# Order of VectorE's work within a part of a graph network's first layer: its additions and next one-hots ahead of its counting work instead of behind it

## The chip, the cores and the metric

The kernel runs on one core of a Trainium2 chip. Its time is the device time of one execution in microseconds (us). Lower is better. The engines are called as in the profile: PE is TensorE (its weight loads are PEld), DVE is VectorE, ACT is ScalarE, POOL is GpSimd and SP is SyncE, which only issues transfers.

## The reference, cut to what matters

A graph of 12,500 nodes with 128 features and 200,000 edges, sorted by destination, goes through a layer norm with ReLU and then three SAGE layers (128 to 256 to 256 to 128 features). Batch norm and ReLU stand between the layers, and the input is added to the result.

```python
def _sage_conv(x, src, dst, Wl, bl, Wr):
    agg = jax.ops.segment_sum(x[src], dst, num_segments=x.shape[0])
    deg = jax.ops.segment_sum(jnp.ones_like(dst, dtype=x.dtype), dst, num_segments=x.shape[0])
    mean = agg / jnp.maximum(deg, 1.0)[:, None]
    return mean @ Wl + bl + x @ Wr
```

The sum over edges is most of the work. The change concerns the stretch in which the first layer's sums are made.

## The kernel before, in words

**Two ways to sum.** Destinations are so skewed that the first nodes get most edges. For them the kernel counts, once, how many edges go from each source to each destination. This table, `edge_count`, is made in `HBS` = 46 strips of 64 destinations. It then multiplies the node features by the counts ("dense"). The remaining edges are walked in tiles of 128: POOL gathers 128 rows of the node table by an indirect DMA into `ring` (line 698), PE multiplies the rows by a 128x32 one-hot matrix of where each edge goes (`sum_part`, line 929), and DVE adds the 32 resulting columns into the sums in `big` (`accumulate`, line 1268).

**Bodies and parts.** In the first layer, 52 bodies of 4 parts of 5 tiles are worked through. `ring` and `onehot` have room for one body. Part g of body i+1 takes the place of part g of body i as soon as PE has multiplied the latter: ACT then copies the next indices (`stage_indices`, line 802), POOL gathers with them, and DVE writes the next one-hots (`hots`, lines 1243 and 1261). PE alternates between two PSUM banks for its products, so its product for a part waits for the additions of the part two before it.

**What rides along.** Each part of the first layer's bodies also carries a slice of other work, named `counting`:

- Bodies 0 to 8: nothing in the parts; DVE and PE make tables between the bodies.
- Bodies 9 to 35 (108 parts): the counts. DVE makes two f16 one-hot matrices for each step, in batches of at most 8 steps (`count_hots`, line 1399, two instructions a batch). They go into 16 slots. PE multiplies them, one matmul a step (`count_edges`, line 943), and ACT copies the result out of PSUM (line 815). Before a batch of slots is overwritten, DVE waits for PE to have done the steps that were in them (`s_count_step`), and PE waits for the batch (`s_count_hot`). There are 2208 steps: the first 8 parts have 48, 24, 20, 16, 14, 14, 12 and 12; then come 4 parts of 24, 8 of 20, 8 of 16, 48 of 24 and 32 of 16.
- Bodies 36 to 51: the dense product (`first_dense`, line 964, in 49 parts, the first of body 36 to the first of body 48) on PE, and the degrees. For these, DVE makes the hots in every second part (`window_degrees`, lines 1290, 1243, 1293 and 1296, in parts 0 and 2), and PE multiplies them in parts 1 and 3 (`sum_degrees`, line 951).

**Order on the engines.** Each engine has its own program, in order, tied to the others by semaphores. In a part, PE does `sum_part` and then its counting matmuls. DVE does its counting one-hots, then loads five window positions into registers (`nodes_of`, line 1271), then the five additions, each waiting for PE's `sum_part` of the same part or for the addition before, and then the next one-hots. In a part g, DVE's `accumulate` waits as follows, and `hots` waits for the same semaphore value:

```python
                if j == 0:
                    dve.wait_ge(s_sum[layer], i * PARTS + (g + 1))
```

The other two layers use `add_parts` with a `counting` that does nothing. An irregular-input branch is not taken with these inputs.

Of the kernel before, what the change touches and what calls it, by code (L numbers as in the profile page):

```python
# [78 lines left out]
def gnn_kernel(nc, x, src, dst, Wl0, bl0, Wr0, g0, b0, Wl1, bl1, Wr1, g1, b1, Wl2, bl2, Wr2, out):  # L79
# [10 lines left out]
    with ctx:  # L90
# [1070 lines left out]
        def _(dve):  # L1161
# [78 lines left out]
            def one_hots(out, numbers, values):  # L1240

                n, w = values.shape[1], numbers.shape[1]
                return V.tensor_tensor(out, numbers.rearrange("p (a w) -> p a w", a=1).to_broadcast([P, n, w]),  # L1243
                                       values.rearrange("p (n a) -> p n a", a=1).to_broadcast([P, n, w]), ALU.is_equal)

            def hots(layer, i, g):
                if not (isinstance(i, int) and i == 0):

                    dve.wait_ge(s_sum[layer], i * PARTS + (g + 1 - PARTS))
                n = PER_PART[layer]  # L1250
                rel = rel_all[:, ds(i * PER_BODY[layer] + (FIRST[layer] + g * n), n)]
                one_hots(onehot[:, g * n:(g + 1) * n, :], iota_row[:, 0:W], rel).then_inc(s_hot[layer], 1)

            def accumulate(layer, i, g, j, node):
                n = PER_PART[layer]
                if j == 0:
                    dve.wait_ge(s_sum[layer], i * PARTS + (g + 1))
                k = g * n + j

                if not (isinstance(i, int) and i == 0 and k == 0):  # L1260
                    dve.wait_ge(s_acc[layer], i * PER_BODY[layer] + k)
                step = part_ps(layer, g, j)
                if layer == 1:
                    sums = big[:, 0:2, ds(node, W)]
                    step = step.rearrange("p (m c) -> p m c", c=W)
                else:
                    sums = big[:, 1 if layer == 0 else 0, ds(node, W)]
                V.tensor_tensor(sums, sums, step, ALU.add).then_inc(s_acc[layer], 1)  # L1268

            def nodes_of(first, count, most):  # L1270
                _, values = nc.values_load_multi_w_load_instructions(  # L1271
                    node_row[0:1, ds(first, count)], engines=[mybir.EngineType.DVE], min_val=0, max_val=most,
                    skip_runtime_bounds_check_because="a window starts at a node or a block, and at most where it ends with the last")
                return values
# [25 lines left out]
            def add_parts(layer, i, counting=lambda g: None, last=False):  # L1300
                n = PER_PART[layer]
                for g in range(PARTS):
                    counting(g)
                    nodes = nodes_of(i * PER_BODY[layer] + (FIRST[layer] + g * n), n, PADDED - W)
                    for j in range(n):
                        accumulate(layer, i, g, j, nodes[j])
                    if not last:
                        hots(layer, i + 1, g)

            def hots_of_first(layer):  # L1310
                for g in range(PARTS):
                    hots(layer, 0, g)
# [93 lines left out]
            def body_0(i, counting):  # L1406
                add_parts(0, i, counting, last=isinstance(i, int) and i == BODIES[0] - 1)
                if isinstance(i, int):
                    if i == 0:
                        say_irregular()  # L1410
                        tables_for_picks()
                        window_nodes()
                    if i == 1:
                        mark_reached()
                    if i == 2:
                        dve.wait_ge(s_steps, 1)
                        link(V.scalar_tensor_tensor(out=tile_row, in0=flat_ps[:, 3 * 512:3 * 512 + STEP_COLS], scalar=1.0,
                                                    in1=tile_row, op0=ALU.max, op1=ALU.add))
                        pick(0)
                    if 3 <= i < 3 + len(STEP_CHUNKS):  # L1420
                        keep_codes(i - 3)
                        if i - 2 < len(STEP_CHUNKS):
                            pick(i - 2)
                    if i == 2 + len(STEP_CHUNKS):
                        link(V.reduce_sum(tally[:, 0:1], tally[:, 2:2 + len(STEP_CHUNKS)], mybir.AxisListType.X))
                        V.tensor_tensor(tally[:, 7:8], tally[:, 1:2], tally[:, 0:1], ALU.subtract).then_inc(s_insides, 1)
                    if i == TABLE_BODIES - 1:
                        dve.wait_ge(s_total, 1)
                        V.tensor_scalar(outside[:, :], ps[:, 3, 0:1], float(EDGES), None, ALU.add).then_inc(s_outside, 1)
# [119 lines left out]
            def sum_edges(layer):  # L1549
                hots_of_first(layer)  # L1550
                dve.wait_ge(s_zero[layer], (CHUNKS + 1) // 2)
                dense_bodies(dve, layer, lambda i, units, last: add_parts(layer, i, last=last))
                dve.wait_ge(s_acc[layer], BODIES[layer] * PER_BODY[layer])
                with if_irregular(dve):
                    dve.wait_ge(s_dense, dense_kept(layer))
                    link(V.memset(big[:, 0:3 - layer, :], 0.0), s_sort)
                    sum_late(layer)
                dve.sem_inc(s_summed, 1)
# [64 lines left out]
```

## Time and profile before

| | before |
|---|---|
| median of 3 runs | 4572.26 us (4563.02 to 4572.82) |
| the profiled execution | 4568.78 us |
| its span in the trace | 4567.0 us |
| mean granted PE clock over the span | 0.852 of full |
| PE, DVE, ACT, POOL busy | 3538.9, 1965.2, 665.2, 3180.7 us |
| first counting one-hots of DVE | 369.48 us into the span |
| last counting matmul of PE begins | 1377.6 us into the span |

### The profile page before, as it was taken

The numbers are of one execution on the slowest core, as the hardware profiler recorded it, in microseconds if no ns is written. First come the engines' busy times: TensorE is split into PE (matmuls) and PEld (weight loads), VectorE is DVE, ScalarE is ACT, GpSimd is POOL, SyncE is SP. The second block draws the span as 40 slices with busy tenths as digits, with TensorE's granted clock in tenths as the row PEclk, the third lists the DMA queues.
The fourth block names the chain that finished last, engine by engine and source line by source line (L and its number), as shares of the span: only waits on it lengthen the run. The fifth ranks groups of instructions, "written<-read, shape, count | busy, mean of one in ns | idle before, by whom it ended". The sixth has DMA issues, their size and how long they took to land.

```text
span 4567.0 us, 62659 instructions
## 1 busy us (share of the span) xinstructions
PE 3538.9 (77%) x16020; PEld 2298.8 (50%) x16020; DVE 1965.2 (43%) x5344; ACT 665.2 (15%) x1712; POOL 3180.7 (70%) x3027
## 2 busy tenths in 40 slices
PE   3356766666668996889999999999885888888876
PEld 1233433333434554776666666666583444444446
DVE  4546867878766777532222222222361222222212
ACT  3001234444440000420000000000030000000002
POOL 2778887777887777037777777777725777777774
PEclk6567878878778996999999999999897888888887
DMA  5212345445569995187677677777669888888886
GB/s 170 65 52 72 121 158 196 189 183 208 227 233 276 290 290 144 74 270 205 203 203 207 199 213 203 203 203 203 206 202 248 214 221 218 214 214 224 213 229 185
DMA packets 928868, 896.10 MB, mean 196 GB/s; under 512 B 62823, under 2 KB 832505, under 8 KB 921754
## 3 DMA queue, kind: packets, MB, share of 16 engines
q1 hardware_dynamic: 819210, 643.90, 47.9%
q0 software_dynamic: 106432, 250.27, 19.0%
q10 hardware_dynamic: 3152, 1.06, 0.1%
q8 instruction: 33, 0.54, 0.0%
q14 instruction: 41, 0.34, 0.0%
HBM read 683.01 MB, written 211.98 MB: 196 GB/s over the span
## 4 chain that ended last, share of the span: by engine, by line
PE 35%; issue 15%; POOL 14%; DMA 12%; DVE 11%; SPq 8%; DVEq 3%; ACT 1%; POOLq 0%; ACTq 0%
POOL ring L698 14%; PE ps L1083 14%; PE ps L929 11%; DMA ring<-table,idx_now 9%; SPq L537 6%; DVE area L1399 5%; PE ps L943 2%; DVE big L1268 2%; PE ps L1125 2%; PE ps L1110 2%; DVEq L1271 2%; DMA table<-area 1%; PE ps L1153 1%; PE ps L1056 1%; PE ps L1063 1%
## 5 line engine op out<-in xcount | busy, mean ns | idle before, releaser
L698 POOL DMA_INDIRECT ring<-table,idx_now x2836 | 3026.7, 1067 | 1051.7 <-issue 924.7
L1268 DVE TENSOR_TENSOR big<-big,ps 128x32 f32 (+1 forms) x2836 | 566.4, 200 | 2205.2 <-PE ps L929 1808.2
L929 PE MATMUL ps<-onehot,ring 128*128 128x32 f32 x7632 | 1023.7, 288 | 495.9 <-DMA ring<-table,idx_now 281.2
L929 PEld LDWEIGHTS ps<-onehot,ring 128*128 128x128 f32 x7632 | 1030.5, 210 | 733.8 <-issue 711.4
L1083 PE MATMUL ps<-area 128*128 128x512 f32 (+1 forms) x2744 | 1380.1, 649 | 25.1 <-DMA area<-table 24.2
L1083 PEld LDWEIGHTS ps<-area 128*128 128x128 f32 x2744 | 553.8, 214 | 564.3 <-issue 539.7
L943 PE MATMUL ps<-area 128*128 128x392 f16 x2208 | 518.2, 395 | 230.1 <-DVE area L1399 228.1
L1399 DVE TENSOR_TENSOR area<-iota_code,area 128x3136 f16<-128x3136 f16 (+4 forms) x568 | 648.8, 1204 | 57.7 <-PE ps L943 53.5
L802 ACT ACTIVATE idx_now<-idx_all 128x5 int32 (+3 forms) x608 | 125.1, 207 | 3034.4 <-PE ps L929 3019.9
L943 PEld LDWEIGHTS ps<-area 128*128 128x128 f16 x2208 | 237.1, 115 | 479.5 <-DVE area L1399 272.0
L815 ACT ACTIVATE big<-ps 128x392 f32<-128x392 f32 x736 | 350.8, 499 | 419.9 <-PE ps L943 418.4
L964 PE MATMUL ps<-big 128*128 128x512 f32 x444 | 203.1, 607 | 22.6 <-DMA big<-table 22.6
L737 POOL MEMSET big<- 128x512 f32 (+2 forms) x50 | 36.2, 725 | 252.7 <-ACT ring L850 252.7
L1243 DVE TENSOR_TENSOR onehot<-iota_row,rel_all 128x160 f32<-128x160 f32 (+1 forms) x608 | 190.5, 315 | 16.2 <-issue 5.0
L964 PEld LDWEIGHTS ps<-big 128*128 128x128 f32 x444 | 82.5, 192 | 115.9 <-issue 109.5
L1125 PE MATMUL ps<-ring,w 128*128 128x256 f32 x392 | 86.9, 385 | 19.8 <-DMA ring<-input 19.8
L1296 DVE TENSOR_SCALAR area<-iota_code,area,wrong 128x98 f16<-128x98 f16 x416 | 94.3, 330 | 4.2 <-DVE wrong L1293 2.0
L1110 PE MATMUL ps<-w,ring 128*128 128x256 f32 x392 | 86.3, 384 | 7.6 <-ACT ring L850 7.6
L1125 PEld LDWEIGHTS ps<-ring,w 128*128 128x128 f32 x392 | 75.8, 194 | 31.2 <-issue 20.5
L1520 DVE BATCH_NORM_STATS2 stats<-big (+2 forms) x196 | 72.8, 414 | 28.5 <-ACT big L835 28.2
L1110 PEld LDWEIGHTS ps<-w,ring 128*128 128x128 f32 x392 | 75.5, 193 | 18.4 <-issue 8.0
L850 ACT ACTIVATE ring<-big,bn_shift,bn_scale 128x512 f32 (+2 forms) x100 | 74.3, 796 | 61.6 <-DMA input<-ring 44.8
(138 smaller groups left out, 1418.7 us busy)
## 6 DMA issues: line engine op xcount, KB each, us to landing
edge_count<-big SPq DMA_DIRECT2D x46, 3136.0 KB
area<-edge_count SPq DMA_DIRECT2D x98, 1472.0 KB
area<-edge_count SPq DMA_DIRECT2D x98, 960.0 KB
big<-edge_count SPq DMA_DIRECT2D x37, 1536.0 KB, 10.0
ring<-table,idx_now POOLq DMA_INDIRECT x2836
area<-table SPq DMA_DIRECT2D x98, 256.0 KB
ring<-input SPq DMA_DIRECT2D x98, 256.0 KB, 2.7
input<-ring SPq DMA_DIRECT2D x48, 512.0 KB, 3.8
```

The costliest lines, as they stand in the source:

```text
L537: sp.dma_start(first_rows[b], tb0[:, ds(unit * 2, 2), :]).then_inc(s_unit[b], 16)
L698: pool.indirect_dma_start(out=ring[:, g * n + j, 0:width], out_offset=None, in_=table[layer][:, :], in_offset=bass.IndirectOffsetOnAxis(ap ...
L815: nc.scalar.activation(count_half[:, half, :, k * GN:(k + 1) * GN], ps[:, 4 + k % 4, 0:CODES].rearrange("p (s n) -> p s n", n=GN), ACT.Cop ...
L929: last = nc.tensor.matmul(to[:, m * W:(m + 1) * W], ring[:, k, m * P:(m + 1) * P], onehot[:, k, :], start=True, stop=True)
L943: nc.tensor.matmul(ps[:, 4 + k % 4, 0:CODES], low_hot[:, slot % SLOTS, :], code_hot[:, slot % SLOTS, :], start=(c == 0), stop=(c == caps[k ...
L964: last = nc.tensor.matmul(first_dense_ps(b)[:, 0:wide].rearrange("p (h c) -> p h c", c=HB), first_rows[g][:, s, :], first_counts[g][:, at ...
L1083: last = nc.tensor.matmul(dense_ps(layer, f, k)[:, 0:(end - h) * HB].rearrange("p (h c) -> p h c", c=HB), unit_rows[b][layer][:, s, f * P: ...
L1110: last = nc.tensor.matmul(ps[:, u, j * HID:(j + 1) * HID], h_stage[:, u, k, j * P:(j + 1) * P], w1[:, 0, k, :], start=(k == 0), stop=(k == 1))
L1125: last = nc.tensor.matmul(ps[:, u, m * CH:(m + 1) * CH], w1[:, 1, k, m * P:(m + 1) * P], own1[:, u, k, :], start=(k == 0), stop=(k == 1))
L1243: return V.tensor_tensor(out, numbers.rearrange("p (a w) -> p a w", a=1).to_broadcast([P, n, w]), values.rearrange("p (n a) -> p n a", a=1 ...
L1268: V.tensor_tensor(sums, sums, step, ALU.add).then_inc(s_acc[layer], 1)
L1399: ins = V.tensor_tensor(hots[:, at:at + count, :].rearrange("p s (n a) -> p s n a", a=2), iota_code[:, 0:w].rearrange("p (b n a) -> p b n ...
```

## The change

In `add_parts`, `counting(g)` is moved from ahead of the loads, additions and next one-hots of part g to behind them. Only DVE's program changes; the programs of PE, ACT, POOL and SP, all waits and all instructions stay the same. For bodies 9 to 35, `counting` is `count_hots`, and for bodies 36 to 51 it is `window_degrees` in parts 0 and 2; elsewhere it does nothing.

```diff
             def add_parts(layer, i, counting=lambda g: None, last=False):
                 n = PER_PART[layer]
                 for g in range(PARTS):
-                    counting(g)
                     nodes = nodes_of(i * PER_BODY[layer] + (FIRST[layer] + g * n), n, PADDED - W)
                     for j in range(n):
                         accumulate(layer, i, g, j, nodes[j])
                     if not last:
                         hots(layer, i + 1, g)
+                    counting(g)
```

## Rows read from the trace of the kernel before

**Rows 1.** Busy time by stage; columns: stretch, length, engines (instructions), clock, DMA share, GB/s

```profile
369.40:434.60 65.20, 49.22 (x240) 29.25 (x240) 55.68 (x98) 9.11 (x23) 53.34 (x39) 0.79 0.15 39
434.60:610.50 175.90, 113.27 (x582) 68.58 (x581) 133.74 (x225) 43.42 (x99) 145.43 (x101) 0.80 0.36 129
610.50:1112.80 502.30, 324.15 (x1641) 183.14 (x1638) 393.16 (x577) 201.33 (x434) 386.00 (x257) 0.83 0.49 187
1112.80:1375.80 263.00, 163.58 (x822) 104.44 (x822) 187.22 (x321) 116.74 (x283) 216.38 (x147) 0.80 0.61 232
1375.80:1728.90 353.10, 326.96 (x1358) 183.02 (x1357) 242.65 (x673) 12.51 (x54) 265.20 (x250) 0.97 1.15 289
```

**Rows 2.** Who waited for whom, stretch 660 to 1112 us, parts of 24 steps

```profile
PE ps L943 <- DVE area L1399: 158.2, 104, 4.0
DVE big L1268 <- issue: 47.7, 22, 2.4
```

**Rows 3.** Who waited for whom, stretch 1201 to 1376 us, parts of 16 steps

```profile
PE ps L929 <- DMA ring<-table,idx_now: 30.4, 5, 6.3
```

**Rows 4.** Timeline, 1000 to 1040 us: start, length, engine, line, operation

```profile
1001.52 4.69 DVE L1399 TENSOR_TENSOR area<-iota_code,area 128x1024 f16<-128x1024 f16 x4
...
1003.97 4.55 PE L943 MATMUL ps<-area 128*128 128x392 f16 x16 [2.08 <-DVE area L1399]
...
1008.86 1.50 DVE L1268 TENSOR_TENSOR big<-big,ps 128x32 f32 x5
...
1010.33 1.20 PE L929 MATMUL ps<-onehot,ring 128*128 128x32 f32 x10
...
1010.63 6.99 DVE L1399 TENSOR_TENSOR area<-iota_code,area 128x1024 f16<-128x1024 f16 x6
...
1019.02 1.20 PE L929 MATMUL ps<-onehot,ring 128*128 128x32 f32 x10
1019.74 1.51 DVE L1268 TENSOR_TENSOR big<-big,ps 128x32 f32 x5 [2.12 <-issue]
...
1021.52 4.69 DVE L1399 TENSOR_TENSOR area<-iota_code,area 128x1024 f16<-128x1024 f16 x4
...
1023.97 4.94 PE L943 MATMUL ps<-area 128*128 128x392 f16 x16 [3.76 <-DVE area L1399]
...
1030.83 1.20 PE L929 MATMUL ps<-onehot,ring 128*128 128x32 f32 x10
```

**Rows 5.** Counting matmuls, one line of the kernel: shortest, median and longest in ns

```profile
L943 PE MATMUL ps<-area x2208: 326/329/535, 373.2 to 1377.6; 128*128 128x392 f16 x184
```

**Rows 6.** Timeline, 1215 to 1255 us, parts of 16 steps

```profile
1223.09 2.00 POOL L698 DMA_INDIRECT ring<-table,idx_now  x1 [0.30 <-issue]
...
1231.85 2.34 PE L929 MATMUL ps<-onehot,ring 128*128 128x32 f32 x10 [6.01 <-DMA ring<-table,idx_now]
...
1234.41 1.51 DVE L1268 TENSOR_TENSOR big<-big,ps 128x32 f32 x5 [3.76 <-PE ps L929]
```

**Rows 7.** Timeline, 1500 to 1530 us, dense product and degrees

```profile
1501.89 1.20 PE L929 MATMUL ps<-onehot,ring 128*128 128x32 f32 x10
...
1503.32 1.51 DVE L1268 TENSOR_TENSOR big<-big,ps 128x32 f32 x5 [2.34 <-PE ps L929]
...
1509.40 1.25 PE L929 MATMUL ps<-onehot,ring 128*128 128x32 f32 x10
...
1522.67 0.89 PE L951 MATMUL ps<-area 128*98 128x128 f16 x13
```

**Rows 8.** Timeline, 1738 to 1760 us, degrees without a dense product

```profile
1742.95 1.08 DVE L1290 TENSOR_SCALAR area<-area,iota_row 128x1664 f16<-128x1664 f32 x1
...
1750.64 1.62 PE L951 MATMUL ps<-area 128*98 128x128 f16 x13 [6.42 <-DVE area L1296]
...
1752.05 2.34 PE L929 MATMUL ps<-onehot,ring 128*128 128x32 f32 x10
...
1754.95 1.28 DVE L1290 TENSOR_SCALAR area<-area,iota_row 128x1664 f16<-128x1664 f32 x1
```

## The prediction

> **What bounds the kernel now.** I read the busy time by stage first, cutting the span where DVE begins the one-hots of another kind of part. The counting bodies 9 to 35 are the first four stretches and last 65.2 + 175.9 + 502.3 + 263.0 = 1006.4 us for 108 parts [rows 1]. There DVE is busy 71 to 85% of the time, PE 62 to 76%, POOL 77 to 83%. No engine is full, so the next view is who waits for whom. In the parts of 24 steps, which take 502.3 / 48 = 10.5 us each, PE waits for the counting one-hots (158.2 us in 104 waits), and DVE waits 47.7 us in 22 waits for nothing but its own issue, ahead of the additions: the register load [rows 1, 2]. In the parts of 16 steps, 263.0 / 32 = 8.2 us each, PE waits for gathered rows [rows 1, 3]. Then comes the timeline, to see who overlaps with whom. PE makes a part's product at 1010.33; DVE begins the same part's counting one-hots at 1010.63 and adds the product at 1019.74, 9.4 us after it was made [rows 4]. The reader is to see that the additions hardly ever wait for PE here, because PE has the product ahead of the counting matmuls. That is why DVE can go on without pause: while PE works off up to 16 slots, DVE adds and starts the next part's one-hots. After them, in bodies 36 to 48, PE is busy 326.96 of 353.1 us at clock 0.97, and is the bound [rows 1].
>
> **What the change does in bodies 9 to 35.** No instruction is added or removed, and none on another engine moves. Let S be PE's product of a part, P its counting matmuls, A the additions, H the next one-hots, C the counting one-hots. PE's order is S P, S P. DVE's was C A H; it becomes A H C. A(g) needs S(g), S(g) stands behind P(g-1) on PE, and P(g-1) needs C(g-1). So after its last batch of C, DVE must wait until PE has worked off all the slots and made S, and only then add; meanwhile nothing for P(g) is made, and PE in turn waits through A, H and the first batch of C. The two engines overlap only inside C and P. The part becomes one chain:
>
> - A and H: from the start of the additions to that of the one-hots, 1010.63 - 1008.86 = 1.77 us [rows 4].
> - The first batch: PE starts 1003.97 - 1001.52 = 2.45 us after DVE (again 2.45 at 1021.52) [rows 4].
> - The matmuls. In these two instances PE had been waiting 2.08 and 3.76 us, as it will in each part now (1.77 + 2.45 is 4.2 us), and 16 of them took 4.55 and 4.94 us [rows 4]. The third batch must wait for slots of the first. From the start of C to the next S, 24 steps took 1010.33 - 1001.52 = 8.81 and 1030.83 - 1021.52 = 9.31 us; I take the mean, 9.06. Without the third batch it is 2.45 + 4.75, less 0.1 because matmul ends are modelled: 7.1. Four steps more at the upper clock add 0.67.
> - S until A can start: 1503.32 - 1501.89 = 1.43 us [rows 7].
>
> So a part takes 1.77 + 9.06 + 1.43 = 12.26 us for 24 steps, 10.3 for 16 and 10.97 for 20. A step fewer than 16 takes off 4.75 / 16 = 0.3: 9.7 for 14 and 9.1 for 12. The 48-step part adds three batches at DVE's pace of 6.99 / 3 = 2.33 [rows 4], 19.3. By stretch, against rows 1:
>
> - First 8 parts: 19.3 + 12.26 + 10.97 + 10.3 + 2 x 9.7 + 2 x 9.1 = 90.4, before 65.2: +25.2.
> - 4 of 24, 8 of 20, 8 of 16: 219.2, before 175.9: +43.3.
> - 48 of 24: 588.5, before 502.3: +86.2.
> - 32 of 16: 329.6, before 263.0: +66.6.
>
> Together +221.3 us. This is net of what goes away: the stalls for the register load fall into the wait for P and S (3.1 us from the end of C to A, against at most about 2.2 for the load), and the waits for rows vanish since the gathers have time: in the last stretch they average 216.38 / 147 = 1.47 us with 0.30 between, 8.9 us for five [rows 1, 6], under 10.3. That cover is thin: a gather beside DVE's one-hots took 2.00 us [rows 6], and five such would be 11.5 us. But the one-hots fill less of a longer part than before. DVE's reads of PSUM sooner release PE's banks sooner, which nobody waits for: costed at nothing, below nothing excluded, because no wait for the banks is among the large ones.
>
> By the Trainium skill (SBUF — State Buffer, on which ops grab the shared pair), a tensor_tensor of DVE should not hold up GpSimd's descriptors, as the page infers; the gather of 2.00 us beside line 1399 disagrees. By the page POOL would leave more room still, and the sum would be the same.
>
> **The bounds of the clock's share.** At the upper level throughout, a matmul goes at half of the 0.327 us that rows 5 show as the common duration. C to S is then 2.45 + 2 x 2.33 + 1.3 = 8.4 us for 24 steps, 6.1 for 16, 6.75 for 20: parts of 11.6, 9.3 and 9.95 us, together +133. At the lower level throughout, matmuls take 0.327 each and S to A 1234.41 - 1231.85 = 2.56 us [rows 5, 6]: parts of 14.6, 12.0 and 13.3 us, together +448. I take the mixture because two instances with nearly this idle time show it.
>
> **Bodies 36 to 51.** In parts 0 and 2, `window_degrees` now starts after A and H. S at 1509.40 lets A start at 1510.83 and the work at 1512.6; it lasts 1750.64 - 1742.95 = 7.7 us, so it ends at 1520.3, and the consumer on PE stands at 1522.67 [rows 7, 8]. With 2.3 us to spare PE's dense product hides it: 0 (if a register load of 2.2 us fell ahead of A it would still do). If that cover were gone, the price would be the excess, twice in each of 12 bodies: a microsecond is 24 us. Where the dense product has ended (some 7 pairs of parts, to the end of body 51) there is no cover. From the end of the work, PE's degree matmuls take 1752.05 - 1750.64 = 1.41, S until A 2.56, A and H 1.7, the work 7.7: 13.4 us, against 1754.95 - 1742.95 = 12.0 us before [rows 6, 8]. The difference is between 0 and 1.4; I take 1.0, +7, less 2 for the additions that no longer stand behind the last of this work. Bodies 0 to 8 and the other layers have no counting in their parts: 0.
>
> **Sum.** 221.3 + 7 - 2 = +226 us on the profiled execution's 4568.8: 4795. Its time was 3.5 below the median of the runs, so 4798.
>
> **Rivals.**
> - *Upper clock.* PE gets the upper level despite pauses of 4 us: +133 + 5, 4710. For it: even after a pause the 16 matmuls take less than the 5.2 us of the lower level. Against it: they take 4.94 us, not 2.6, after 3.76 us of waiting [rows 4].
> - *Lower clock.* PE never leaves the lower level, as its work comes in pieces: +448 + 5, 5025. For it: a median of 0.329 us, and 2.34 us for S after a wait of 6.01 [rows 5, 6]. Against it: the products after the counting matmuls take 1.20 [rows 4]. The Trainium skill (TensorE: Matmul & The Clock Gate, "What's actually happening") has the clock throttled by default and released by activity; with the new pauses that rule speaks for this rival.
> - *The gathers set the pace.* If the chain were shorter than POOL's pace, nothing would change: 4572. That needs parts of 16 steps at 8.2 us and of 24 at 10.5, where even the upper clock gives 9.3 and 11.6.
> - *Faster.* The register load ahead of A moves out of DVE's way. It cost 47.7 us in 22 waits [rows 2]; for 26 of the 52 parts of 24 steps that is 26 x 2.17 = 56 us: 4516. It decides only if A's new wait for P and S is shorter than what the load cost, about 1.1 us a part; I find 3.1.
>
> **How the numbers follow.** Mixed clock 0.64 (4740 to 4890), upper 0.14, lower 0.10, gathers 0.05, faster 0.04, and 0.03 for something slower outside these. I predict 4798. The range of 4700 to 4920 holds the first two and leaves the rest out. A difference of 0.2% (9 us) is about what can be told from no change: faster 0.04, same 0.05, slower 0.91.
>
> **What would show it.** In the profile after: the counting stretch lasts about 1228 us instead of 1006; parts of 24 steps 12.3 us, of 16 steps 10.3; DVE's largest waits are additions waiting for PE's product (line 929), some 3 us in every part; PE waits about 4 us for each first batch; POOL waits for ACT's indices in most parts; the register load no longer shows; PE still at 0.97 in the dense bodies. It would be wrong if PE's clock settles at one level, or if the degree work in bodies 36 to 48 comes late for PE.

## The result and the profile after

The changed kernel took 4814.41 us at the median (4811.03 to 4816.63) against 4572.28 us before: a ratio of 1.0534, interval 1.0516 to 1.0552. The prediction was 4798 us, 226 us of loss; the measured loss is 242 us. The profiled execution took 4811.03 us with a span of 4809.2 us, 242.2 us more than the span of before.

First, the same view as [rows 1]: busy time by stage, each stretch cut where DVE begins the one-hots of another kind of part. Columns: stretch, length, busy time of PE, PEld, DVE, ACT and POOL with their instructions, granted clock, DMA share, GB/s.

```profile
375.10:467.40 92.30, 55.79 (x240) 30.91 (x240) 56.25 (x96) 9.61 (x24) 64.97 (x52) 0.70 0.17 50
467.40:690.40 223.00, 133.69 (x584) 74.71 (x584) 135.13 (x225) 43.93 (x100) 130.38 (x101) 0.71 0.28 100
690.40:1286.30 595.90, 356.82 (x1632) 194.09 (x1632) 396.87 (x577) 200.89 (x432) 314.42 (x241) 0.77 0.41 156
1286.30:1615.50 329.20, 186.14 (x832) 106.74 (x832) 187.84 (x322) 127.44 (x288) 205.49 (x161) 0.67 0.50 188
1615.50:1977.40 361.90, 333.04 (x1408) 187.38 (x1408) 248.82 (x695) 10.16 (x49) 267.02 (x247) 0.97 1.13 285
```

The reader is to see three things. The four counting stretches have grown from 65.2, 175.9, 502.3 and 263.0 us to 92.3, 223.0, 595.9 and 329.2. DVE's work has not (396.87 us in the third, before 393.16 us). PE's has, with the same work, since its clock fell from 0.83 to 0.77 in the third stretch and from 0.80 to 0.67 in the fourth. The dense stretch that follows is at 0.97, as before.

Who waited for whom, 720 to 1280 us, parts of 24 steps (total us, times, longest), to be held against [rows 2]:

```profile
PE ps L943 <- DVE area L1399: 224.2, 77, 4.6
POOL ring L698 <- ACT idx_now L802: 209.1, 45, 4.9
DVE big L1268 <- PE ps L929: 127.3, 45, 3.1
```

In 45 parts DVE's additions now wait 127.3 / 45 = 2.83 us for PE's product, the new wait. PE waits for DVE in turn, and POOL for the indices of the next gathers, 45 times. Before, the additions' large wait was the register load; it is gone from the list.

The timeline of the same kernel, 1150 to 1192 us, shows one whole part (start, length, engine, line):

```profile
1160.50 1.51 DVE L1268 TENSOR_TENSOR big<-big,ps 128x32 f32 x5 [2.87 <-PE ps L929]
...
1162.28 4.69 DVE L1399 TENSOR_TENSOR area<-iota_code,area 128x1024 f16<-128x1024 f16 x4
...
1164.73 4.45 PE L943 MATMUL ps<-area 128*128 128x392 f16 x16 [4.46 <-DVE area L1399]
...
1167.70 2.39 DVE L1399 TENSOR_TENSOR area<-iota_code,area 128x1024 f16<-128x1024 f16 x2 [0.72 <-PE ps L943]
...
1170.15 1.50 PE L943 MATMUL ps<-area 128*128 128x392 f16 x8 [0.97 <-DVE area L1399]
...
1171.49 1.20 PE L929 MATMUL ps<-onehot,ring 128*128 128x32 f32 x10
...
1172.92 1.52 DVE L1268 TENSOR_TENSOR big<-big,ps 128x32 f32 x5 [2.83 <-PE ps L929]
```

This is the chain of the prediction: from the additions to the one-hots 1.78 us, from the start of the one-hots to the product 9.21 (2.45 of it until PE has the first batch), from the product to the next additions 1.43. Together 12.42 us, where 12.26 were forecast. PE stands idle 4.46 us at the head of this part, 4.39 and 4.46 at the heads of its neighbours.

In the parts of 16 steps (timeline, 1455 to 1495 us) the cycle is 10.24 us, from 1460.27 to 1470.51, where 10.3 were forecast:

```profile
1460.27 1.51 DVE L1268 TENSOR_TENSOR big<-big,ps 128x32 f32 x5 [3.77 <-PE ps L929]
...
1464.50 4.75 PE L943 MATMUL ps<-area 128*128 128x392 f16 x16 [4.46 <-DVE area L1399]
...
1470.51 1.50 DVE L1268 TENSOR_TENSOR big<-big,ps 128x32 f32 x5 [3.77 <-PE ps L929]
```

In these parts PE waited for gathered rows before [rows 3]; now the gathers are on time and the chain sets the pace.

### The profile page after: what moved, and what is told of

It reads as the page before. It is cut to its first block, busy times and chain, and to the rows that moved or that the text cites. A ratio compares the mean times of both kernels' runs of the same rounds, so it can differ in the third digit from the quotient of the medians.

```text
span 4809.2 us, 62646 instructions
## 1 busy us (share of the span) xinstructions
PE 3623.5 (75%) x16020; PEld 2322.8 (48%) x16020; DVE 1969.7 (41%) x5344; ACT 674.2 (14%) x1712; POOL 3088.4 (64%) x3027
## 4 chain that ended last, share of the span: by engine, by line
PE 47%; issue 12%; DVE 11%; POOL 10%; DMA 8%; SPq 7%; DVEq 4%; ACT 1%; POOLq 0%; ACTq 0%
PE ps L1083 14%; PE ps L929 13%; PE ps L943 11%; POOL ring L698 9%; SPq L537 6%; DMA ring<-table,idx_now 5%; DVE area L1399 5%; DVE big L1268 3%; DVEq L1271 2%; PE ps L1125 2%; PE ps L1110 2%; DMA table<-area 1%; PE ps L1153 1%; PE ps L1056 1%; DVEq L1268 1%
## 5 line engine op out<-in xcount | busy, mean ns | idle before, releaser
L698 POOL DMA_INDIRECT ring<-table,idx_now x2836 | 2934.3, 1035 | 1376.6 <-issue 893.0
L929 PEld LDWEIGHTS ps<-onehot,ring 128*128 128x128 f32 x7632 | 1014.0, 207 | 589.3 <-issue 567.5
L929 PE MATMUL ps<-onehot,ring 128*128 128x32 f32 x7632 | 1001.7, 285 | 360.7 <-DMA ring<-table,idx_now 197.2
L943 PE MATMUL ps<-area 128*128 128x392 f16 x2208 | 618.5, 457 | 508.0 <-DVE area L1399 507.4
L943 PEld LDWEIGHTS ps<-area 128*128 128x128 f16 x2208 | 267.8, 128 | 825.7 <-DVE area L1399 464.3
```

The source lines that it names most:

```text
L698: pool.indirect_dma_start(out=ring[:, g * n + j, 0:width], out_offset=None, in_=table[layer][:, :], in_offset=bass.IndirectOffsetOnAxis(ap ...
L929: last = nc.tensor.matmul(to[:, m * W:(m + 1) * W], ring[:, k, m * P:(m + 1) * P], onehot[:, k, :], start=True, stop=True)
L943: nc.tensor.matmul(ps[:, 4 + k % 4, 0:CODES], low_hot[:, slot % SLOTS, :], code_hot[:, slot % SLOTS, :], start=(c == 0), stop=(c == caps[k ...
```

## The experiments

The kernel before was measured again beside the experiments (medians of 4564.08 us for 1 to 4, 4566.97 for 5 to 7 and 4565.45 for 8 and 9), and each ratio is against that. For each kernel, besides its ratio, the *counting stretch* is given: from the first to the last start of a counting matmul in the profiled execution. Before, it is 1377.6 - 373.2 = 1004.4 us [rows 5]; in the changed kernel 1612.3 - 377.4 = 1234.9 us, 230.5 more:

```profile
L943 PE MATMUL ps<-area x2208: 326/531/534, 377.4 to 1612.3; 128*128 128x392 f16 x184
```

The median matmul now takes 531 ns, before 329.

**1. Only the counts behind.** Each part has two places for its work, phase 0 ahead of the additions and phase 1 behind them. The counting one-hots are made in phase 1 alone; the degree work is done in phase 0 alone, by the same kind of test where it is called.

```diff
                 for g in range(PARTS):
+                    phase[0] = 0
                     counting(g)
...
                         hots(layer, i + 1, g)
+                    phase[0] = 1
+                    counting(g)
...
             def count_hots(groups, step, hb, half, caps):
+                if phase[0] == 0:
+                    return
```

> Only the counting one-hots (bodies 9 to 35) go behind the additions; the degree work stays ahead of them. The chain theory puts nearly all of the loss here: the counting matmuls began 4.2 us later and ended 235 us later in the changed kernel, so about 4805 us. The rival, that the degree work is what comes late for PE, gives close to 4572.

Measured: 4803.39 us, ratio 1.0528 (1.0510 to 1.0546). The counting stretch is 1612.4 - 377.6 = 1234.8 us, that of the whole change to 0.1 us. The loss sits in the counting bodies.

**2. Only the degrees behind.** The same, with the two kinds of work exchanged.

> Only the degree work of bodies 36 to 51 goes behind the additions. The chain theory gives about 10 us, all of it in the last three bodies, where no dense product hides it: 4582 us. If the degree work were late for PE in bodies 36 to 48 too, it would be tens of us more.

Measured: 4573.45 us, ratio 1.0020 (1.0010 to 1.0030), so 9 us of loss: small, but the interval leaves out 1. The profiled execution was the longest of the ten, 14 us above the median, so its rows are used for where the loss sits and not for its size. In the rows of the degree matmuls before (first) and in this kernel (second), the last one starts at 1826.7 and 1837.1 us, while counting ended 1.2 us earlier here:

```profile
L951 PE MATMUL ps<-area x416: 217/219/344, 1412.4 to 1826.7; 128*98 128x128 f16 x139
```

```profile
L951 PE MATMUL ps<-area x416: 217/219/345, 1410.1 to 1837.1; 128*98 128x128 f16 x139
```

The last dense matmul starts at 1737.6 us here against 1739.5 before. So bodies 36 to 48 lose nothing, and the loss is behind them, as forecast. The ratios of 1 and 2 add up to that of the whole change (5.28% + 0.20%, against 5.34%, within the intervals).

**3. Next one-hots ahead, additions behind.** This asks whether the additions' work or the wait for PE makes the loss.

```diff
                 for g in range(PARTS):
+                    if not last:
+                        hots(layer, i + 1, g)
                     counting(g)
                     nodes = nodes_of(...)
                     for j in range(n):
                         accumulate(layer, i, g, j, nodes[j])
-                    if not last:
-                        hots(layer, i + 1, g)
```

> Next one-hots ahead of the counting work, additions behind it. The one-hots wait for the same product of PE as the additions, so DVE still stands idle through PE's tail, but the 1.5 us of additions leave the chain. The chain theory gives 12.4 - 1.5 = 10.9 us for a part of 24 steps and 8.8 for one of 16, so 108 x 1.5 = 160 us less than the changed kernel: 4655 us. If only the additions' own wait mattered, it would be as before, 4572; if the place of the one-hots alone mattered, as the changed kernel, 4814.

Measured: 4619.09 us, ratio 1.0115 (1.0099 to 1.0132). The counting stretch is 1426.3 - 381.2 = 1045.1 us, 190 less than in the changed kernel, where 160 were expected. Merely moving the 0.33 us one-hots ahead costs about 1%, because they wait for the same product (the degree work stands behind them here too; behind one-hots and additions it was 0.2% in 2). Most of the loss is gone with the additions' work off the chain. The wait (timeline, 900 to 925 us):

```profile
902.20 0.33 DVE L1243 TENSOR_TENSOR onehot<-iota_row,rel_all 128x160 f32<-128x160 f32 x1 [1.34 <-PE ps L929]
...
904.91 1.50 PE L943 MATMUL ps<-area 128*128 128x392 f16 x8 [2.88 <-DVE area L1399]
```

PE's wait is 2.88 us here instead of 4.46, and after it the first 8 matmuls take 1.50 us, the time of the upper clock level. This does not hold in every part: in the next one, 16 matmuls take 5.26 us after a wait of 3.19. The granted clock is 0.82 from 700 to 1100 us and 0.80 from 1170 to 1400, where the changed kernel has 0.77 in its parts of 24 steps and 0.67 in those of 16. That is where the additional 30 us come from as I read it, though this kernel does not test the clock by itself. The next one does.

**4. The changed kernel with PE kept at work.** Each counting part has 20 matmuls on constants ahead of its counting matmuls, into a bank that is free then; the results are not used.

```diff
+            low_fill, code_fill = iota_code[:, 0:P], iota_code[:, 0:CODES]
+            FILL = 20
+
             def count_edges(groups, step, hb, half, caps):
                 n = sum(caps[k] for k in groups)
+                for _ in range(FILL):
+                    nc.tensor.matmul(ps[:, 2, 0:CODES], low_fill, code_fill, start=True, stop=True)
```

> The changed kernel with 20 matmuls of 392 columns on constants in each counting part, ahead of the part's counting matmuls, into a PSUM bank that is free then; their results are never used. They stand where PE waits 4.4 us for the first batch and take 3.3 us at the upper clock. If a part of the loss is PE's lower clock after its waits, parts go to 11.6 us (24 steps) and 9.3 us (16 steps): about 95 us less, 4720 us. If the clock has no part in it, no gain, or a loss where the 20 take longer than the wait: 4814 or more.

Measured: 4710.46 us, ratio 1.0319 (1.0301 to 1.0336). More work for PE takes 104 us off the changed kernel's 4814.41; by the two ratios, each against the kernel before as measured beside it, it is 2.15%, or 98 us. The counting stretch is 1508.9 - 380.5 = 1128.4 us, 106.5 less than in the changed kernel. Busy time by stage, 720 to 1180 us, then the timeline of one part, the fillers standing at line 939 and the counting matmuls at line 948:

```profile
720.00:1180.00 460.00, 351.92 (x2150) 206.70 (x2150) 323.75 (x478) 166.71 (x359) 295.02 (x199) 1.00 0.44 168
```

```profile
1002.57 1.20 PE L929 MATMUL ps<-onehot,ring 128*128 128x32 f32 x10
...
1003.60 3.48 PE L939 MATMUL ps<-iota_code 128*128 128x392 f16 x20
1004.00 1.51 DVE L1273 TENSOR_TENSOR big<-big,ps 128x32 f32 x5 [2.83 <-PE ps L929]
...
1008.23 1.50 PE L948 MATMUL ps<-area 128*128 128x392 f16 x8 [1.15 <-DVE area L1404]
...
1010.53 1.50 PE L948 MATMUL ps<-area 128*128 128x392 f16 x8 [0.81 <-DVE area L1404]
...
1012.84 1.50 PE L948 MATMUL ps<-area 128*128 128x392 f16 x8 [0.80 <-DVE area L1404]
1014.17 1.20 PE L929 MATMUL ps<-onehot,ring 128*128 128x32 f32 x10
1015.21 3.48 PE L939 MATMUL ps<-iota_code 128*128 128x392 f16 x20
1015.61 1.51 DVE L1273 TENSOR_TENSOR big<-big,ps 128x32 f32 x5 [2.83 <-PE ps L929]
```

The clock is at 1.00, every batch of 8 takes 1.50 us, and the part 1015.61 - 1004.00 = 11.6 us, exactly the bound that the prediction gave for the upper level. DVE's wait is unchanged at 2.83 us. So of the 230.5 us, 106.5 go when the clock is held up in the pauses, and 124 stay, the lost overlap with PE at the upper level. The kernel before had a clock of 0.79 to 0.83 in this stretch and was not run with such fillers. So 124 us is not the price of the overlap at equal clocks, and whether the fillers would gain there too is open.

**5. Only the last batch behind.** The batches of a part are divided between the two places; the degree work stays ahead.

```diff
                     count = min(n - done, LANES - at % LANES)
+                    if (phase[0] == 1) != (done + count == n):
+                        done += count
+                        continue
```

> In each counting part only the last batch of counting one-hots goes behind the additions and next one-hots; the batches before it stay ahead, the degree work too. In a part of 24 steps the last batch must wait for slots that PE frees only after the product the additions wait for, so the additions fill a wait instead of making one. The chain theory says that a loss needs PE to be without a batch while DVE waits, and here it has one: no slower than before, and if DVE's waits for slots were worth something, parts of 24 steps at 9.5 instead of 10.5 us: 4520 to 4572 us, I say 4545. A rival, that any additions ahead of counting work cost the wait for PE, gives a loss of 50 us or more.

Measured: 4541.43 us, ratio 0.9942 (0.9928 to 0.9955), the fastest of all kernels here. The counting stretch is 1343.0 - 374.3 = 968.7 us, 36 less than before. In its timeline (878 to 900 us; the one-hots are at line 1407) two parts follow each other in 9.6 us:

```profile
885.68 1.50 DVE L1268 TENSOR_TENSOR big<-big,ps 128x32 f32 x5
...
887.50 4.69 DVE L1407 TENSOR_TENSOR area<-iota_code,area 128x1024 f16<-128x1024 f16 x4
...
889.94 2.79 PE L943 MATMUL ps<-area 128*128 128x392 f16 x8 [2.62 <-DVE area L1407]
...
895.31 1.52 DVE L1268 TENSOR_TENSOR big<-big,ps 128x32 f32 x5
```

The additions of these two parts have no idle time ahead of them: neither a wait for the product nor for the register load. From 600 to 1090 us they wait 30.6 us in 21 waits for the product and never for the load. The gain lies in the parts of 24 steps. Measured from the product of one part to that of the next, their 48 take 459.4 us (615.4 to 1074.8), 9.57 each, where before they took 491.3 (621.3 to 1112.6), 10.24 each. The parts of 16 steps take 8.42 us, before 8.36. So the edit of the study, done for one batch in place of all, gains.

**6. All but the first batch behind.**

```diff
+                    if (phase[0] == 0) != (done == 0):
+                        done += count
+                        continue
```

> In each counting part only the first batch of counting one-hots stays ahead of the additions; the others go behind. PE has one batch of at most 8 steps (1.3 to 2.6 us) to work on while DVE waits 1.4, adds 1.8 and makes the next batch 2.4 us. The chain theory gives parts of 24 steps of 9.3 to 10.5 us and leaves the parts of 16 at the pace of the gathers: 4530 to 4590 us, I say 4555. The rival that any additions ahead cost the wait gives about half of the loss, 4690.

Measured: 4564.10 us, ratio 0.9994 (0.9985 to 1.0003), no difference. One batch of at most 8 steps in PE's hands while DVE waits and adds is enough to undo the whole loss; the rival, half of the loss, falls.

**7. The register load by itself.**

```diff
-                    counting(g)
                     nodes = nodes_of(...)
+                    counting(g)
```

> The order of before, but the five window positions are loaded into registers ahead of the counting one-hots instead of ahead of the additions. It prices the load by itself. In the order of before, DVE waits 2.2 us for it in every second part of 24 steps. If its place makes the price, the parts of 24 steps lose that and gain the load's 1.2 us elsewhere: 4550 to 4590 us. If the load is free wherever it finds DVE waiting, 4516.

Measured: 4572.53 us, ratio 1.0011 (1.0002 to 1.0020). The load is not free, it only changes its victim. Waits at 750 to 1000 us, of before and then of this kernel:

```profile
DVE big L1268 <- issue: 28.3, 13, 2.3
```

```profile
DVE area L1399 <- issue: 26.7, 23, 1.7
```

**8. The changed kernel with PE's product one part earlier.** DVE's order is that of the change. PE makes the product of part g+1 ahead of the counting matmuls of part g, which were ahead of it.

```diff
             def body_0(i, counting):
                 for g in range(PARTS):
-                    sum_part(0, i, g)
+                    if g + 1 < PARTS:
+                        sum_part(0, i, g + 1)
+                    elif not (isinstance(i, int) and i == BODIES[0] - 1):
+                        sum_part(0, i + 1, 0)
                     counting(g)
...
+            sum_part(0, 0, 0)
             first_bodies(pe, body_0, count_edges, tail)
```

> DVE in the order of the changed kernel (additions, next one-hots, counting work), but PE makes the product of a part one part earlier: ahead of the counting matmuls of the part before, not behind them. If the loss is that the additions wait for a product that stands behind the tail of PE's counting matmuls, that wait goes: DVE adds right after its one-hots, PE still has up to 16 slots to work off, and the loss of the counting bodies vanishes: parts of 24 steps at 9.3 to 10.5 us, of 16 at the gathers' pace, 4520 to 4580 us, I say 4555. If the loss came from DVE's order by itself, or from PE's clock alone, it stays near 4814.

Measured: 4550.68 us, ratio 0.9965 (0.9951 to 0.9978). The counting stretch is 1362.6 - 380.4 = 982.2 us. In the timeline, 900 to 925 us, the additions are at line 1272:

```profile
909.80 1.20 PE L929 MATMUL ps<-onehot,ring 128*128 128x32 f32 x10
...
910.40 6.99 DVE L1403 TENSOR_TENSOR area<-iota_code,area 128x1024 f16<-128x1024 f16 x6
...
917.31 1.50 DVE L1272 TENSOR_TENSOR big<-big,ps 128x32 f32 x5
917.45 1.50 PE L943 MATMUL ps<-area 128*128 128x392 f16 x8 [0.80 <-DVE area L1403]
```

PE makes the product at 909.80, the additions start as the one-hots end, and PE still has its last batch to do. DVE's order is the one that lost 5.3%, with a loss turned into a small gain by a change on PE alone. This is the strongest evidence for the cause: it is not DVE's order by itself, but that the product it waits for stands behind PE's tail.

**9. Both 5 and 8.**

> The kernel with only the last batch of counting one-hots behind the additions (0.994 of the time before), with PE's product one part earlier too. The chain theory says that its additions hardly wait any more, so little is left to gain: parts of 24 steps at DVE's own 9.0 to 9.4 us, parts of 16 at the gathers' pace: 4515 to 4545 us, I say 4535. A rival, that the last batch behind gained by something other than filled waits, adds both gains in full: below 4515.

Measured: 4551.46 us, ratio 0.9964 (0.9952 to 0.9977): no gain over 8, and less than 5 alone. My 4535 was too low. In the parts of 16 steps (waits, 1150 to 1350 us), PE now waits for gathered rows, and behind it DVE for slots:

```profile
DVE area L1411 <- PE ps L943: 49.3, 12, 5.6
PE ps L929 <- DMA ring<-table,idx_now: 43.8, 12, 5.3
```

In 5 the wait for rows is 1.9 us there (1150 to 1340 us). From product to product, the parts of 24 steps take 9.57 us in 5, 9.60 in 8 and 9.52 here, so the two edits take the same time away and do not add up. The parts of 16 take 8.42, 8.54 and 8.80 us, which is 12 of the 16.6 us by which the counting stretch is longer here (1366.4 - 381.1 = 985.3 us) than in 5. A product placed earlier also needs its rows earlier, and it holds up the counting matmuls that stand behind it. That this is the cause of the difference to 5 is read from the waits and was not tested.

## Why the prediction was right, point by point

- **The chain.** Shown by 8 (the wait taken away by PE's order), 6 (a batch of work left for PE), 3 (a loss from the one-hots' wait, with the additions off the chain) and the rows of a part. Its links were forecast as 1.77, then 2.45 and the matmuls (9.06 together), and 1.43; measured 1.78, 9.21 and 1.43.
- **The counting bodies.** Forecast 90.4 + 219.2 + 588.5 + 329.6 = 1227.7 us, measured 92.3 + 223.0 + 595.9 + 329.2 = 1240.4 us. The mis-sized terms are the part of 24 steps, 12.42 us and not 12.26, which is 8 us over 52 parts, and the part of 20 steps, 11.4 us on average from product to product and not 10.97, which is 4 us over 9 parts. Of two instances I took the mean (8.81 and 9.31 us), and the pause of the changed kernel, 4.46 us, is nearer to the instance after the longer pause.
- **The clock's share.** I took a mixture between +133 (upper level) and +448 (lower). The mixture was right, and 4 shows the upper bound at 124 us of counting stretch; its 4710 us is also what the rival of the upper clock forecast, so that rival had the price right, and only its condition, the upper level despite the pauses, did not hold. That two instances gave the 4.75 us of 16 matmuls to the hundredth is luck in part: in single parts of the changed kernel they take from 4.1 to 5.2 us (690 to 1615 us). The rival that PE never leaves the lower level falls: the product takes 1.20 to 1.30 us in 100 of 106 parts. The Trainium skill (TensorE: Matmul & The Clock Gate, "What's actually happening") has the clock throttled by default and released by activity. The trace agrees in direction: 0.77 and 0.67 with the pauses, 1.00 with matmuls in their place.
- **A reading that was wrong.** I took the 0.329 us of [rows 5] for a matmul at the lower level, and counted it in favour of that rival. It is the duration at the upper level: in 4, at a clock of 1.00, the counting matmuls have

```profile
L948 PE MATMUL ps<-area x2208: 326/329/341, 380.5 to 1508.9; 128*128 128x392 f16 x184
```

At the lower level a matmul lasts 0.53 us, the median of the changed kernel. Matmuls overlap, so their spacing is less than their duration. At the upper level 8 take 1.50 us, so they start (1.50 - 0.33) / 7 = 0.17 us apart. After a pause, at the lower level, the weight loads of the changed kernel follow each other at 0.33 us:

```profile
1165.03 0.15 PEld L943 LDWEIGHTS ps<-area 128*128 128x128 f16 x1 [0.17 <-issue]
1165.36 0.15 PEld L943 LDWEIGHTS ps<-area 128*128 128x128 f16 x1 [0.18 <-issue]
1165.68 0.15 PEld L943 LDWEIGHTS ps<-area 128*128 128x128 f16 x1 [0.18 <-issue]
```

The sums of the prediction needed spacings and used 0.327 us and half of it. That the duration at one level is near the spacing at the other is a coincidence, and it kept the error out of both bounds. Read rightly, the median of before was evidence against the lower clock.

- **The degrees.** Under the dense product the work of one part ends at 1749.05 + 2.97 = 1752.0 us in the changed kernel and PE's degree matmuls start at 1754.21: 2.2 us to spare, where 2.3 were forecast. Behind it, I had 13.4 us for a pair of parts and measured 2015.33 - 2001.83 = 13.5, but then took 1.0 us of loss a pair and not 1.4, and 2 us off for the last additions. The term was +5 and measured 243.0 - 231.4 = 11.6 us (from the start of the last dense matmul, 231.4 us later than before, to that of the last degree matmul, 243.0 us later). That is 6.6 us more than forecast. The last dense matmul starts 231.4 us later where the counting bodies were to give 221.3, 10 us more. The two make up the miss.
- **What was put at nothing.** POOL's pace did not bind: it waits for indices 45 times between 720 and 1280 us, once a part. The gathers had 241 x 1.30 us of work in 595.9 us. The cover that the prediction called thin held, since only one of a part's five gathers took 2.00 us beside the one-hots; the others of the part at 1161.40 us took 0.94 to 1.40.
- **The faster rival.** The register load was hidden as I said, but 7 shows that its 56 us were not to be had by moving it. In 5 the additions no longer wait for it, and the parts of 24 steps are 32 us shorter in all; but in 8 they are as short (9.60 us) while DVE still waits for the load (13.5 us in 8 waits, 750 to 1000 us). So it is not shown that the load is what 5 gained.

## What to carry to other kernels

When two engines feed each other through a ring of slots, the slack is the work that one still holds while the other waits. Before moving an instruction ahead, ask where on the other engine the thing it waits for is queued, and what the other engine has to do meanwhile. If a wait must come first, leave at least one batch ahead of it (6), or let the other engine make the awaited result ahead of its backlog (8); placed where the engine waits in any case, the same move gains (5).

## What the runs showed of the hardware that was not expected

- Useless work made the kernel faster. Twenty matmuls a part, 2160 in all, took 106.5 us off the counting stretch. With them PE's granted clock was 1.00 from 720 to 1180 us, where pauses of 4.46 us in a cycle of 12.4 us had left it at 0.77.
- The clock repeats in a steady pattern: in the parts of 16 steps, neighbouring cycles of the changed kernel each have 16 matmuls in 4.75 us and a product in 1.20, within 10.24 us.
- The register load (line 1271) has no fixed price. In the order of before it took from 0.59 to 4.65 us, median 2.48, in the parts of 24 steps; in the changed kernel, where DVE soon stands idle behind it, 1.05 to 1.70, median 1.19.
